# One Perceiver and Mamba layer on one core: u turned by four square transposes a block, band matmuls of 512 columns, scan rows by sequence and state, and a reordered opening of the scan

## What is computed

```python
xz = einsum('bld,pd->blp', norm(x), in_proj_w)          # 512 channels xi, 512 channels z
xi, z = xz[..., :DI], xz[..., DI:]
xc = silu(conv4(xi) + conv_b)
xp = einsum('bli,pi->blp', xc, x_proj_w)                # 1 + 16 + 16 columns
delta = softplus(xp[..., :1] * dt_w[:, 0] + dt_b)
Bp, Cp = xp[..., 1:17], xp[..., 17:]
dA = exp(delta[..., None] * -exp(A_log))
dB = delta[..., None] * Bp[:, :, None, :] * xc[..., None]
# for each of 64 tokens: h = dA_t * h + dB_t ; y_t = sum over 16 states of h * C_t
y = (y + xc * D_skip) * silu(z)
x = x + einsum('bli,di->bld', y, out_proj_w)
```

## Time and profile before

| | us |
|---|---|
| runs | 496.21, 491.97, 495.17 |
| median | 495.17 |
| profiled execution, whole | 497.46 |
| its span (first to last instruction) | 495.7 |
| mean granted TensorE clock | 0.947 |

### The profile page before, as it was taken

How to read it: one execution, slowest core, us unless ns; L and a number is a source line. 1 busy time by engine, 2 the same in 40 slices (tenths; PEclk the granted TensorE clock), 3 DMA queues, 4 the chain that set the end, 5 groups by cost and what they waited for, 6 DMA issues and landing times. The chain is left out here.

```text
span 495.7 us, 9213 instructions
## 1 busy us (share of the span) xinstructions
PE 427.2 (86%) x3138; PEld 296.8 (60%) x3138; DVE 367.6 (74%) x770; ACT 253.5 (51%) x547; POOL 297.8 (60%) x326
## 2 busy tenths in 40 slices
PE   4899999999999795945879989999889988979764
PEld 2566767767667452525566657577668765747433
DVE  1566877768689888115577997598878799996894
ACT  1356557565874442558314546548741835126463
POOL 0245446464464624032896758799998899973810
PEclk9999999999999789977599999999999999997997
DMA  8911101011000000039000000066100000000001
GB/s 290 412 67 45 44 0 45 1 44 45 2 0 2 2 0 0 2 106 258 1 1 1 0 1 26 1 144 159 39 1 0 2 1 0 1 3 0 12 32 44
DMA packets 22770, 22.73 MB, mean 46 GB/s; under 512 B 1058, under 2 KB 20258, under 8 KB 22212
## 3 DMA queue, kind: packets, MB, share of 16 engines
q1 hardware_dynamic: 22164, 21.65, 14.0%
q10 hardware_dynamic: 560, 0.49, 0.3%
HBM read 21.02 MB, written 1.12 MB: 45 GB/s over the span
## 5 line engine op out<-in xcount | busy, mean ns | idle before, releaser
L1645 POOL TENSOR_TENSOR both<-both 128x1024 f32<-128x1024 f32 x64 | 150.1, 2361 | 34.1 <-DVE both L1363 34.0
L1363 DVE TENSOR_TENSOR_SCAN both<-both,ps 128x1024 f32<-128x1024 f32 x64 | 144.1, 2276 | 29.3 <-PE ps L634 28.2
L990 ACT ACTIVATE both<-delta,a_neg 128x504 f32<-128x504 f32 x128 | 79.2, 702 | 39.5 <-DVE both L1363 39.4
L1599 POOL TENSOR_SCALAR both<-both,rden 128x256 f32<-128x256 f32 x128 | 61.9, 498 | 51.2 <-DVE rden L1211 51.1
L634 PE MATMUL ps<-both 64*128 64x256 f32 x512 | 75.2, 414 | 13.3 <-POOL both L1633 9.7
L644 PE MATMUL ps<-con,both 128*128 128x128 f32 x512 | 71.6, 284 | 6.7 <-POOL both L1645 6.7
L889 ACT ACTIVATE both<-both,negmax 128x256 f32<-128x256 f32 x128 | 63.3, 498 | 22.4 <-DVE negmax L1204 22.4
L644 PEld LDWEIGHTS ps<-con,both 128*128 128x128 f32 x512 | 56.3, 143 | 29.2 <-issue 15.2
L634 PEld LDWEIGHTS ps<-both 64*128 64x128 f32 x512 | 46.1, 192 | 34.1 <-issue 17.8
L1204 DVE CUSTOM_DVE_ANT_0 both<-ps,both 128x256 f32<-128x256 f32 x128 | 46.7, 419 | 15.0 <-PE ps L403 14.8
L442 PE MATMUL ps<-both 128*128 128x512 f32 x64 | 36.1, 695 | 6.5 <-DMA both<-in_ctx_t 6.5
(11 more groups left out here) (133 smaller groups left out, 649.7 us busy)
## 6 DMA issues: line engine op xcount, KB each, us to landing
both<-bounce SPq DMA_DIRECT2D x16, 512.0 KB, 5.7
both<-in_ctx_t SPq DMA_DIRECT2D x8, 512.0 KB, 3.4
both<-in_wg SPq DMA_DIRECT2D x1, 1024.0 KB, 10.3
both<-in_wu SPq DMA_DIRECT2D x1, 1024.0 KB, 12.3
both<-in_wd SPq DMA_DIRECT2D x1, 1024.0 KB, 14.2
win_sb<-in_win SPq DMA_DIRECT2D x1, 1024.0 KB, 16.6
...
```

Source lines behind the costliest of these rows:

```text
L990: act.activation(da[sl % 2].rearrange("p (a n s t) -> p a n s t", a=GT, n=HN, s=2)[:, :, n, :, 1:L], delta[:, idx % RING_X].rearrange("p ( ...
L1363: dve.tensor_tensor_scan(h_sb[:, hu % RING_H], da[e.slot % 2][:, e.tt * HU:(e.tt + 1) * HU], bank(2 * (hu % 2), 2), 0.0, ALU.mult, ALU.add ...
L1599: pool.tensor_scalar(s, s, rden[:, u, q:q + 1], 1.0, ALU.mult, ALU.mult).then_inc(normed, 1)
L1645: pool.tensor_tensor(h, h, cb[:, e.nh, e.tt], ALU.mult).then_inc(g_ready, 1)
```

## The change

1. **u turned.** `turn_u` makes four 128x128 transposes into one bank, with 64-row halves of the result holding the two sequences of a piece, where before 16 matmuls with 64 columns of weights wrote each sequence to both row halves. So `ut` is half as large, one turn and one copy stand for two, and they are placed anew in the loops: VectorE copies block 1 at hu 5, 4 at 28, 5 at 35, 6 at 41, 7 at 50; TensorE turns block 4 at hu 27, and `in_proj(1, 7)` moves from hu 29 to hu 26.
2. **B turned.** `turn_b` makes four matmuls of 16 columns for 16 of 8.
3. **Inflow.** Two matmuls of 512 columns, one for each sequence, on row half s of `ut` and `bd`, each into one whole bank, where before four of 256 columns were written in runs of 64. Elements of h, da and dB lie by sequence, then state, then token.
4. **Weigh.** Output to `g_sb`, a ring of 3 of its own, in the order state, sequence, token, from h in the new order; it waits for accumulate(hu-3). `h_sb` becomes a ring of 3; scan(hu) waits for weigh(hu-3).
5. **Opening.** ScalarE makes softplus of block 0 alone, then `decay_first`: slot 0's exponentials in two sets of 8 with 252 elements, the first for halves 0 and 1; the other three softplus come after slot 1. u of block 0 is made by VectorE. GpSimd makes all 8 spread_b of group 0 before weigh(0). seed(0) and seed(1) come behind inflow(1) and inflow(2). The last scan_in is at hu 6 instead of 7.
6. The feed-forward's `f_h` and `f_hi` lie in `xnt`, which is done with by then; GpSimd waits once for the last in_proj.

TensorE at the start of the scan, before: L587 is turn_b, L598 turn_u, L613 the seeds, L634 inflow, L644 accumulate, L486 scan_in.

The diff, cut to what the sections here speak of:

```diff
-RING_H, RING_X = 4, 5
+RING_H, RING_G, RING_X = 3, 3, 5
...
-        h_sb = both[:, 20480:24576].rearrange("p (k n) -> p k n", k=RING_H)
-        ut = both[:, 24576:26624].rearrange("p (i s d) -> p i s d", i=2, s=SG)
+        h_sb = both[:, 20480:23552].rearrange("p (k n) -> p k n", k=RING_H)
+        g_sb = both[:, 23552:26624].rearrange("p (k n) -> p k n", k=RING_G)
+        ut = both[:, 26624:27648].rearrange("p (i t d) -> p i t d", i=2, t=GT)
...
-                for s in range(4):
-                    at = (half * 4 + s) * L
-                    for r in range(2):
-                        mm = pe.matmul(bank(k)[L * r:L * (r + 1), s * P:(s + 1) * P],
-                                       u_sb[:, i % 2, at:at + L], ident, start=True, stop=True)
+                for tt in range(GT):
+                    mm = pe.transpose(bank(k)[:, tt * P:(tt + 1) * P], u_sb[:, i % 2, tt * P:(tt + 1) * P], ident)
...
                 for s in range(2):
-                    for r in range(2):
-                        out_v = bank(2 * (hu % 2) + r).rearrange("p (n s t) -> p n s t", s=2, t=L)
-                        mm = pe.matmul(out_v[:, :, s], ut[L * r:L * (r + 1), e.idx % 2, 2 * e.tt + s],
-                                       bd[L * r:L * (r + 1), e.nh, e.tt, s * HN // 2 * L:(s + 1) * HN // 2 * L],
-                                       start=True, stop=True, skip_group_check=True)
+                    mm = pe.matmul(bank(2 * (hu % 2) + s), ut[L * s:L * (s + 1), e.idx % 2, e.tt],
+                                   bd[L * s:L * (s + 1), e.nh, e.tt], start=True, stop=True)
...
-            seed(0)
-            seed(1)
             for hu in range(NHU):
                 inflow(hu)
+                if hu == 1:
+                    seed(0)
+                if hu == 2:
+                    seed(1)
...
                 if hu == 26:
-                    turn_u(4, 0, 6, (z_sb, NC + 2))
+                    in_proj(1, 7, 6, (z_sb, NC + 2))
                 if hu == 27:
-                    turn_u(4, 1, 7, (z_sb, NC + 3))
-                if hu == 29:
-                    in_proj(1, 7, 6, (ut_dve, 5))
+                    turn_u(4, 7, (z_sb, NC + 3))
...
+            def decay_first(half):
+
+                act.wait_ge(da_zero, count(1))
+                act.wait_ge(delta_ready, count(1))
+                tts = slice(GT // 2 * half, GT // 2 * (half + 1))
+                for n in range(HN):
+                    act.activation(da[0].rearrange("p (a s n t) -> p a s n t", a=GT, n=HN, s=2)[:, tts, :, n, 1:L],
+                                   delta[:, 0].rearrange("p (a s t) -> p a s t", a=GT, s=2)[:, tts, :, 1:L],
+                                   ACT.Exp, scale=a_neg[:, 0, n:n + 1]).then_inc(da_ready if half else da_first, 1)
...
-            slot(0)
+            decay_first(0)
+            decay_first(1)
             slot(1)
+            softplus(0, range(1, NC))
             slot(2)
...
-                dve.wait_ge(y_acc, count(hu - RING_H + 1))
+                dve.wait_ge(g_ready, count(hu - RING_H + 1))
...
+            dve.tensor_tensor(u_sb[:, 0], delta[:, 0], xc[:, 0], ALU.mult).then_inc(u_first, 1)
+            copy_ut(0, 6)
...
-                h = h_sb[:, hu % RING_H]
-                pool.tensor_tensor(h, h, cb[:, e.nh, e.tt], ALU.mult).then_inc(g_ready, 1)
+                pool.wait_ge(y_acc, count(hu - RING_G + 1))
+                pool.tensor_tensor(g_sb[:, hu % RING_G].rearrange("p (n s t) -> p s n t", n=HN, s=2),
+                                   h_sb[:, hu % RING_H].rearrange("p (s n t) -> p s n t", n=HN, s=2),
+                                   cb[:, e.nh, e.tt].rearrange("p (n s t) -> p s n t", n=HN, s=2), ALU.mult
+                                   ).then_inc(g_ready, 1)
...
-            u_of(0, 0)
-            spread_b(0, 0, 1)
+            for b in range(1, NH * GT):
+                spread_b(0, b // GT, b % GT)
             for hu in range(NHU - 1):
                 weigh(hu)
-                if hu < NH * GT - 2:
-                    spread_b(0, (hu + 2) // GT, (hu + 2) % GT)
```

More of the change, by code:

```diff
@@ L149, in build @@
         winv = sb("winv", [P, 3])
-        both = sb("both", [P, 26624])
+        both = sb("both", [P, 27648])
         def first_use(at, n):
@@ L969, in copy_pr, with softplus @@
                 act.activation(bsb, bank(k), ACT.Copy).then_inc(bsb_ready, 1)
-            def softplus(g):
+            def softplus(g, cs):
                 act.wait_ge(dt_loaded, 16 * (g + 1))
-                act.wait_ge(u_ready, count(g * NC))
-                for c in range(NC):
+                act.wait_ge(u_ready, count(g * NC - 1))
+                for c in cs:
                     act.activation(delta[:, ring_x(g, c)], dtb[:], ACT.Softplus,
@@ L1032, in _ @@
             silu_gates(0)
-            softplus(0)
+            softplus(0, [0])
             act.wait_ge(a_ready, 1)
@@ L1048, in _ @@
                 silu_xc(1, c)
-            copy_ut(3, 0, 6)
-            for n in range(4):
-                decay(5, n)
-            copy_ut(3, 1, 6)
-            for n in range(4, HN):
-                decay(5, n)
+            copy_ut(3, 6)
+            slot(5)
             copy_pr(1, 7)
@@ L1057, in _ @@
             copy_gates(1, 0, 7)
-            softplus(1)
+            softplus(1, range(NC))
             copy_gates(1, 1, 6)
@@ L1101, in _ @@
             silu_gate(0)
[L1102 removed]
+            act.wait_ge(u_ready, count(NG * NC - 1))
             act.wait_ge(db_ready, count(NHU))
```

128 lines of the change are left out of this document (59 added, 69 removed).

## The result

| | before | changed |
|---|---|---|
| median, us (range, runs) | 493.57 (491.9 to 496.21, 4) | 481.54 (479.39 to 482.45, 4) |
| ratio | | 0.9723 (0.9681 to 0.9766) |
| profiled execution, its span | 497.46, 495.7 | 482.13, 480.3 |
| mean granted clock | 0.947 | 0.956 |

A forecast was written before the change was run, and what follows sets the result against it. GpSimd sets the pace from 329.7 to 381.9 us; before that no engine is full and chained waits bound. Terms -4.7 - 9.2 - 0.95 - 0.65 = -15.5 give 482.0 from the profiled execution, 479.7 from the median; forecast 481, range 474 to 489.

The forecast's parts named there:

- Opening: Up to scan(0): shorter softplus, u, turn and copy, seeds no longer in front of inflow; scan(0) at 225.1, 4.7 us earlier.
- Scan(0) to scan(10): Waits for spread_b go, a wait at turn_u(1) comes; 31.4 us instead of 40.6, 9.2 less (7.7 to 10.7).
- The new wait at turn_u(1): At hu 4 TensorE stands from 235.3 until GpSimd's u(1) is ready at 238.4; the largest new wait.
- The branch without it: Scan(0) to scan(10) with TensorE's clock staying at the upper level behind its pause: scan(10) at 255.1.
- The middle: Scan(10) at 256.5, between 255.1 at the upper clock and 258 if the clock falls: 9.2 us less.
- Scan(10) to scan(28): Shorter turns: 1.0 less before scan(19), 0.8 before scan(22); in_proj(1,7) 0.85 more before scan(27); sum -0.95 us.
- Scan(28) to the end: GpSimd paces, so fewer turns are worth nothing; one copy less at hu 49 gives -0.65 us.
- The edits priced at nothing: Wide inflow, contiguous PSUM writes, weigh's third dimension and own output, and the new rings: each taken as 0 us.
- rival 2: Weigh costs 0.1 to 0.25 more, or wide inflow partly loses overlap: +3.5 to +8.8, 484 to 490 us; chance 0.12.
- rival 3: Slower than before: weigh with the third dimension bounds throughout; from about 2.9 us a weigh, above 500 us; chance 0.03.
- Rival 1: Only scan(0) comes earlier; scan(0) to scan(10) keeps its 40.6 us; 6.3 us left, 489 to 491; chance 0.12.
- Rival 4: Clock stays up and ScalarE's short exponentials are cheap: scan(10) at 254, 476 to 478 us; lower edge of the forecast.

The follow-up runs named there:

- e3: The changed kernel with the seven later spread_b of group 0 put back behind the weighs; 489.28 us.
- e8: The changed kernel with u of blocks 6 and 7 made by VectorE (at hu 36 and 39) instead of GpSimd; 478.92 us.
- e6: The changed kernel with in_proj(1, 7) moved back from hu 26 to hu 29; 480.44 us.
- e5: The changed kernel with every turn of u made four times over (16 transposes, same result); 483.78 us.
- e1: The kernel before with the reordered opening alone; turns, inflow, weigh and rings stay old; 484.46 us, ratio 0.9767.

## Why the prediction was right, point by point

**Opening, forecast 4.7, measured 3.98.** The chain of the prediction was the right one; three terms were too small. u on VectorE took 0.96 us, not 0.7: 0.28 with its gap. The inflow starts 0.25 us after its copy ends. And scan(0) starts 2.38 us after the inflow, not 2.11. The 0.7 was the right duration for an undisturbed VectorE: in e3, where GpSimd stands idle then, the same operation is

```profile
219.47 0.69 DVE L1479 TENSOR_TENSOR u_sb<-delta,xc 128x512 f32<-128x512 f32 x1 [5.39 <-ACT delta L963]
```

and it took 0.89 to 1.62 us in the kernels that have spread_b running beside it. It goes the other way too: in the opening of each of those kernels just one spread_b, one that runs beside VectorE's u, takes 1.49 or 1.50 us where the others take about 1.05, and in e3 none does. The changed kernel's (ns, shortest, median and longest):

```profile
L1627 POOL TENSOR_TENSOR both<-con,bt x16: 1041/1050/1494, 213.8 to 341.1; 128x512 f32<-128x512 f32 x16
```

So the edit that is worth most, the early spread_b, lengthened the one beside it, and the prediction had priced the two apart. *The Trainium skill ("GPSIMD Engine Reference", Specifications) says that GpSimd shares its SBUF interfaces with VectorE, and that instructions of VectorE with two SBUF inputs contend with it. The trace agrees: 0.69 alone, 0.89 to 2.86 beside GpSimd's work, while the scan, which reads one operand from PSUM, keeps its 2.277.*

ScalarE's branch was sized well: 16 exponentials of 252 elements in 6.44 us, 0.397 apart against the forecast 0.4. The first eight end at 220.54 + 7 x 0.397 + 0.488 = 223.8, so TensorE's branch decided alone.

**Scan(0) to scan(10), forecast 9.2 (7.7 to 10.7), measured 8.26.** Both parts of the argument held, the waits that go and the wait that comes. Without the waits for spread_b the lead grows by 6.0 up to scan(4), and e3 shows that they are the cause. The new wait at turn_u(1) was put at about 3 us and is 3.06. The prediction left open whether the clock falls behind it, gave scan(10) 255.1 without and 258 with, 2.9 apart, and took the middle. In its profile the clock fell, so the branch to hold against the 8.26 is the one with the fall, 7.7. The branch without it, 10.6, is to be held against e8, which gained 10.93. Each is right within 0.6 us, and so is the price of the fall: 2.9 forecast, 2.56 to 2.73 measured for 6.8 us at the lower level, and 1.49 for 3.4. The middle, 9.2, describes neither execution; as a forecast of a median it is fair, for a reason that the prediction didn't give: the fall does not happen in every execution.

**Scan(10) to scan(28), forecast 0.95, measured 0.72.** I count to scan(27), the last that the terms name. (Scan(28) itself leads by 13.56, but GpSimd, which paces from there on, doesn't: weigh(28) leads by 13.01.) The lead is 12.24 at every scan up to scan(18), as forecast. scan(19) gains 1.04 (1.0). scan(22) gains 0.35, not 0.8: this term was mis-sized. The timeline of the changed kernel, to be held against the earlier trace rows:

```profile
292.87 0.96 PE L586 MATMUL ps<-con,yz 128*128 128x16 f32 x8
...
310.23 1.88 PE L503 MATMUL ps<-win_sb,xnt 128*128 128x512 f32 x4
```

Eight records of 16 columns take 0.96 us, where 32 of 8 columns took 1.11. I had scaled by the count. The source views give the length of one record (ns, shortest, median and longest): of turn_b and of a transpose in the changed kernel, then of turn_b in the kernel before:

```profile
L586 PE MATMUL ps<-con,yz x16: 182/262/263, 212.1 to 293.6; 128*128 128x16 f32 x16
```

```profile
L598 PE MATMUL ps<-con,u_sb x32: 272/273/446, 220.3 to 381.9; 128*128 128x128 f32 x32
```

```profile
L587 PE MATMUL ps<-con,yz x64: 202/203/224, 213.3 to 308.3; 128*64 128x8 f32 x64
```

So the new records start (0.96 - 0.18) / 7 = 0.11 us apart, the same as transposes with eight times as many moving columns, (0.60 - 0.27) / 3 = 0.11; both have 128 columns of weights. The old ones, with 64, start (1.11 - 0.20) / 31 = 0.03 apart. With 128 columns of weights, then, up to 128 moving columns made no difference. That it is the weight loads that set this pace would fit, but no run tests it.

in_proj(1, 7) at hu 26 costs 0.67 (forecast 0.85) where a turn stood before, and e6, where nothing stands there, shows 1.0.

**Scan(28) to the end, forecast 0.65, measured 0.49.** GpSimd full for 52 us: yes. e5 shows that longer turns of TensorE cost only 0.5 there, and e8 that two u less on GpSimd leave 0.6 us at the end. One copy less at block 7, the whole of the 0.65, gave scan(50) 0.6 us and left 0.34 by weigh(52).

**The edits priced at nothing.** Weigh 2.364 for 2.361; four records of inflow in 1.13 us as eight before (e1's 1.14). So rival 2 falls, and rival 3 with it. Rival 1 fell with the 8.26 us that went between scan(0) and scan(10). Rival 4, the clock staying up, came in e8, with the opening of the changed kernel: there scan(10) comes 36.2 us after dt, where the rival's 254 is 34.5 us after it. The rule of the Trainium skill on non-contiguous PSUM patterns ("SBUF — State Buffer", Door 1) would have had inflow shorter now; it is not, with 1.13 us at the upper level for 1.13, and 2.08 at the lower for 2.08.

**The sum.** Forecast 15.5; measured from dt 13.45, so the steps together were 2 us too hopeful. With the branch that happened, 7.7 for 9.2, the sum is 14.0 and 0.55 too much: most of the miss is the fall that was counted by half. The profiled execution's whole is right within 0.2 us (482.13 for 482.0) because two pieces that belong to no step went the same way: 1.14 us ahead of dt and 0.8 behind weigh(63). They are of the size by which executions of one kernel differ, and should not be counted for the reasoning. The median is near for a like reason: 481 was 14.2 us below the median of the time, 495.17, and 481.54 is 12.0 below 493.57. That it came within 0.6 us is luck; that the gain is 12 to 15 us is not. None of the signs of being wrong came: weigh is below 2.5 us, VectorE doesn't wait for ScalarE at scan(8), and from scan(28) to weigh(63) it takes 108.6 us, before 108.5.
